# A three-layer graph network with an expert layer on one core: the last layer's work placed anew, two edge banks in place of three, and a bank for each half of an early slot's hidden product

## The reference, cut to what matters

```python
xn = layernorm(x)
h = xn
for l in range(3):
    agg = segment_sum(h[src], edge_type * N + dst, 8 * N).reshape(8, N, 256)
    h = act_l(einsum('rnd,rde->ne', agg, W[l]) + h @ root[l] + bias[l])   # relu, relu, sigmoid
x = x + h + linear_attention(xn)                                        # 4 heads of 32
y = layernorm(x)
top_p, top_idx = top_k(softmax(y @ Wr + br), 2)                          # 8 experts
yn = layernorm_no_affine(y)
e(y) = gelu((yn * ln_g[e] + ln_b[e]) @ W1[e] + b1[e]) @ W2[e] + b2[e]    # 256 -> 1024 -> 256
out = x + sum over the 2 chosen experts of weight * e(y)
```

## Time and profile before

| | us |
|---|---|
| median of 3 runs (3805.47 to 3815.09) | 3810.72 |
| the profiled execution | 3800.47 |
| its span, first to last instruction | 3798.7 |
| PE busy in the span | 2900.7 (76%) |
| POOL busy in the span | 2397.5 (63%) |
| DVE busy in the span | 1179.5 (31%) |
| ACT busy in the span | 447.0 (12%) |

### The profile page before, as it was taken

How to read it: one execution, slowest core, us unless ns; L and a number is a source line. 1 busy time by engine, 2 the same in 40 slices (tenths; PEclk the granted TensorE clock), 3 DMA queues, 4 the chain that set the end, 5 groups by cost and what they waited for, 6 DMA issues and landing times.

```text
span 3798.7 us, 51045 instructions
## 1 busy us (share of the span) xinstructions
PE 2900.7 (76%) x16228; PEld 2552.1 (67%) x16228; DVE 1179.5 (31%) x2813; ACT 447.0 (12%) x1220; POOL 2397.5 (63%) x2537
## 2 busy tenths in 40 slices
PE   3878777877778888888888778787767777777791
PEld 3776766776666676677666567776666666667791
DVE  5232223222232223222322233333332333333312
ACT  1000000000000000000000010122121211212230
POOL 5777777777757777777776677755445554543005
PEclk9888888898888778877878777798888888888896
DMA  7444444444443333333333333555444454544653
GB/s 175 133 146 132 133 146 133 132 136 143 133 131 110 108 108 109 108 108 108 109 107 100 116 105 105 161 167 160 143 139 159 142 160 137 156 147 133 216 187 112
DMA packets 272287, 511.76 MB, mean 135 GB/s; under 512 B 60237, under 2 KB 177119, under 8 KB 272032
## 3 DMA queue, kind: packets, MB, share of 16 engines
q0 software_dynamic: 120864, 330.20, 29.8%
q1 hardware_dynamic: 150000, 178.85, 14.8%
q10 hardware_dynamic: 1296, 1.24, 0.1%
HBM read 453.68 MB, written 56.42 MB: 134 GB/s over the span
## 4 chain that ended last, share of the span: by engine, by line
POOL 45%; PE 25%; issue 20%; DVE 4%; DVEq 2%; DMA 1%; ACT 1%; ACTq 1%; POOLq 0%; SPq 0%
POOL arena L590 44%; PE bank L1584 6%; PE bank L1530 4%; PE bank L1599 3%; PE bank L1643 3%; PE bank L1639 2%; PE bank L1777 2%; PE bank L1787 2%; POOL arena L655 1%; ACT arena L777 1%; PE bank L1523 1%; DVE arena L1193 1%; DVEq L1228 1%; DMA arena<-rows_dram,arena 0%; PE bank L1521 0%
## 5 line engine op out<-in xcount | busy, mean ns | idle before, releaser
L590 POOL DMA_INDIRECT arena<-rows_dram,arena x2396 | 2268.8, 947 | 906.7 <-issue 751.9
L1639 PE MATMUL bank<-arena 128*128 128x128 f32 x4836 | 1082.2, 331 | 436.0 <-DMA arena<-rows_dram,arena 374.9
L1639 PEld LDWEIGHTS bank<-arena 128*128 128x128 f32 x4836 | 855.3, 223 | 636.9 <-DMA arena<-rows_dram,arena 469.3
L1278 DVE TENSOR_TENSOR arena<-arena,bank 128x256 f32 x807 | 340.4, 422 | 2226.3 <-PE bank L1643 2123.2
L1643 PE MATMUL bank<-arena 128*128 128x128 f32 x4836 | 798.7, 310 | 0.0
L1643 PEld LDWEIGHTS bank<-arena 128*128 128x128 f32 x4836 | 732.1, 226 | 0.0
L1530 PE MATMUL bank<-arena 128*128 128x256 f32 x2400 | 600.3, 390 | 0.0
L1530 PEld LDWEIGHTS bank<-arena 128*128 128x128 f32 x2400 | 445.4, 198 | 49.2 <-issue 0.5
L1584 PE MATMUL bank<-arena 128*128 128x128 f32 x1152 | 220.2, 370 | 255.7 <-DVE arena L1152 171.0
L1584 PEld LDWEIGHTS bank<-arena 128*128 128x128 f32 x1152 | 207.7, 279 | 264.9 <-issue 264.9
L1211 DVE TENSOR_TENSOR arena<-bank,arena 128x1408 f32<-128x1408 f32 x222 | 355.3, 1603 | 13.0 <-issue 13.0
(11 more groups left out here) (204 smaller groups left out, 1373.0 us busy)
## 6 DMA issues: line engine op xcount, KB each, us to landing
arena<-in_L_ffn_W_dram SPq DMA_DIRECT2D x112, 512.0 KB, 4.3
arena<-in_L_ffn_W_dram SPq DMA_DIRECT2D x44, 1024.0 KB, 6.2
arena<-rows_dram,arena POOLq DMA_INDIRECT x2418, 2.8
xs_dram<-zrow SPq DMA_DIRECT2D x25, 1152.0 KB, 5.6
arena<-xs_dram SPq DMA_DIRECT2D x56, 128.0 KB, 2.1
xs_dram<-arena SPq DMA_DIRECT2D x56, 128.0 KB, 2.7
rows_dram<-arena SPq DMA_DIRECT2D x50, 128.0 KB
arena<-in_L_gnn_weights_dram SPq DMA_DIRECT2D x6, 1024.0 KB, 8.8
```

The costliest lines, as they stand in the source:

```text
L590: nc.gpsimd.indirect_dma_start(out=gath[:, slot, :], out_offset=None, in_=rows_dram[l], in_offset=bass.IndirectOffsetOnAxis(ap=idx_ring[:, ...
L1278: nc.vector.tensor_tensor(acc, acc, bank[EDGE_BANKS[q % 3]][:, 0:KD * WC].rearrange("p (k r n) -> p k r n", k=KD, r=REL), ALU.add).then_in ...
L1639: nc.tensor.matmul(bank[EDGE_BANKS[q % 3]][:, 0:WC], gath[:, slot, 0:P], onehot[:, slot, :], start=first, stop=last)
```

## The change

Four things are changed in the last layer, and one in all layers.

1. The tables place the work elsewhere. DVE's numbers now count groups (0 to 10, and 11 for behind the last), and its work stands ahead of that group's addition, no longer behind a tile's.
2. The last layer uses edge banks 0 and 1 in turn. Bank 2 becomes the bank of h1, bank 6 stays that of h0, and each half waits only for the same half of the slot before.
3. The output product of c = 0 goes to the left half of bank 5 and that of c = 1 to the right; the router's and the counts' results move from bank 5 to the turn bank 4. The waits follow.
4. `router` and `route` run in the same span as the node (behind tile 30, ahead of group 10), `dealt` and `route_pos` early in the next span.
5. In every layer the window offsets of a span are loaded into DVE's registers 4, 4 and 3 at a time, where 11 were loaded at once.

```diff
-STAGE, LAST_STAGE, POST, TURN, BACK = 4, 11, 17, 23, 26
+STAGE, LAST_STAGE, POST, TURN, BACK = 4, 11, 14, 23, 26
-X2, YN, XN2, DEV1, DEV2, YBACK, YTURN, ROUTE = 20, 23, 26, 21, 24, 28, 27, 1
+X2, YN, XN2, DEV1, DEV2, YBACK, YTURN, ROUTE = 5, 6, 7, 19, 19, 29, 27, 30
...
-RT, RT_MM, RT_POS = 5, 7, 11
-PICK, LAST_PICK = (14, 17), (13, 13)
-PLACE = (dict(turn=0, scale=2, h0=4, h1=8, out=16, bias=20), dict(turn=17, scale=20, h0=22, h1=25, out=29, bias=32))
+RT, RT_MM, RT_POS = 10, 2, 3
+PICK, LAST_PICK = (3, 4), (4, 4)
+LOADS = 4
+PLACE = (dict(turn=2, scale=0, h0=8, h1=15, out=22, bias=8), dict(turn=19, scale=6, h0=22, h1=29, out=32, bias=11))
...
-        E_HID, E_OUT = 6, 5
+        E_HID, E_OUT = (6, 2), 5
+        router_o = bank[TURN_BANK][:, D:D + EXP]
+        dealt_o = bank[TURN_BANK][:, D + 2 * EXP:D + 4 * EXP]
+        early_o = [bank[E_OUT][:, c * D:(c + 1) * D] for c in range(2)]
...
+        def turned_ahead(u):
+            return sum(at["turn"] < u for at in PLACE)
+        def edge_bank(l, s, q):
+            return bank[EDGE_BANKS[(q + s.par) % 2 if l == LAYERS - 1 else q % 3]]
...
@@ DVE, a span
+                            if q % LOADS == 0:
+                                n = min(LOADS, groups - q)
+                                wins += nc.values_load_multi_w_load_instructions(
+                                    win_row[0:1, bass.ds(SG * s.m + q, n)], engines=(dve.engine,), min_val=0, max_val=RING - 1,
...
+                            beside(q)
                             for u in us[:-1]:
                                 key(u)
                             wait(dve, "group_mm", g + 1)
                             wait(dve, "tile_add", g)
                             acc = agg[:, :, :, bass.ds(wins[q], WN)]
-                            nc.vector.tensor_tensor(acc, acc, bank[EDGE_BANKS[q % 3]]...
+                            nc.vector.tensor_tensor(acc, acc, edge_bank(l, s, q)...
-                                beside(u)
...
+                        beside(groups)
@@ PE
-            def early_turn(k, c, y):
+            def early_turn(k, c, y, signal):
                 s = 2 * k + c
                 pe.wait_ge(s_xe[c], 16 * (k + 1))
                 wait(pe, "e_back", s)
-                wait_apart(pe, "y_out", y)
+                wait(pe, "y_out", y)
+                wait_apart(pe, signal, y)
...
-                wait_apart(pe, "e_act", 2 * s + h)
+                wait_apart(pe, "e_act", 2 * s + h - 1)
...
-                                    wait(pe, "tile_add", GROUPS * l if is_first(s) and q < 3 else g - 1 if q < 2 else g - 2)
+                                    if final:
+                                        wait(pe, "tile_add", GROUPS * l if is_first(s) and q < 2 else g - 1)
+                                    else:
+                                        wait(pe, "tile_add", GROUPS * l if is_first(s) and q < 3 else g - 1 if q < 2 else g - 2)
```

More of the change, by code:

```diff
@@ L1227, in span @@
                         groups = -(-tiles // GT)
[L1228 to L1234, removed]
+                        wins = []
@@ new lines, in beside @@
+                        def beside(q):
+                            if final and early(s) is not None:
+                                for c in range(2):
+                                    if q == places(s)[c]["scale"]:
+                                        early_scale(early(s), c)
+                                    if q == places(s)[c]["bias"]:
+                                        early_bias(early(s), c, early_o[c])
+                            if not is_first(s) and q == READY:
+                                whole(l, t, (s.i,) if not s.par else (), GROUPS * l + SG * s.m + q)
+                            if not is_first(s) and not is_last(s) and q == ZERO:
+                                clean(l, t, place_of(t, s.par))
+                            if final and not is_first(s) and not is_last(s):
+                                if q == X2:
@@ L1235, in beside @@
                                     x2_node(t)
-                                if final and u == YN:
+                                if q == YN:
                                     y_node(t)
-                                if final and u == XN2:
+                                if q == XN2:
                                     xn2_node(t, 1 - s.par, t - 1)
[L1240 to L1244, removed]
+                                if q == RT:
+                                    route(t)
@@ L1245, in beside @@
+                            if final and not (is_first(s) or is_int(s.m, 1)) and q == RT_POS:
+                                route_pos(s.m - 2, s.par, s.m - 3)
                             if final and picks(s) is not None:
                                 for c in range(2):
-                                    if u == (LAST_PICK if is_last(s) else PICK)[c]:
+                                    if q == (LAST_PICK if is_last(s) else PICK)[c]:
                                         pick_slot(2 * picks(s) + c)
[L1249 to L1253, removed]
-                                        early_bias(early(s), c, early_o)
@@ L1255, in beside @@
-                            if l == 0 and u == PREP["bias"]:
+                            if l == 0 and q == PREP["bias"]:
                                 bias_in(s.m)
-                            if l == 1 and not is_first(s) and not is_last(s) and u == MIX_ADD:
+                            if l == 1 and not is_first(s) and not is_last(s) and q == MIX_ADD:
                                 mix_node(t)
```

81 lines of the change are left out of this document (37 added, 44 removed).

## The result

The median of the changed kernel's runs is 3463.18 us (3461.70 to 3463.78, and one run of 3543.67 that the comparison leaves out) against 3809.24 us before on the same chip: ratio 0.9089, 95% interval 0.9071 to 0.9107. The forecast was 3515 us in a range from 3450 to 3650. The change took away 346 us where 295 were forecast; the profiled execution has a span of 3460.7 us against 3798.7.

What follows compares the result with a forecast made beforehand. PE was taken to be held up by short chains through DVE and ACT, POOL following. (89.3 + 4) / 2 = 46.7 us a span; 45 + 794 = 839 for 18 intervals, 295 less: 3515 us, range 3450 to 3650.

Steps and rivals of the forecast that it cites:

- The scaled rows: Last layer, rows of c = 1 scaled ahead of group 6: PE's wait of 12.1 us a span goes.
- A bank for each half: Hidden product, last layer: h1 no longer waits for the gelu of h0; 3.1 us a span go.
- Router, counts, positions: Span ends and starts, last layer: PE's 2.0 us a span for counts go; POOL's 13.3 for `route_pos` shrink.
- Two edge banks: Edge additions, last layer: DVE's piles of work fit under PE's products; cost taken as 0.
- Rival C: DVE's piles ahead of groups 3 to 7 uncovered, PE waits: 69 us a span, 3895 us, slower; chance 0.05.
- Rival B: Last layer: half of PE's 17.6 us of waits remains, 57 us a span, 3690 us; chance 0.10.
- The loop's turn: DVE's 6.0 us stall at the loop's branch stays: 4.9 us a turn added, plus 3 for the lower clock.
- The gathers: POOL, last layer: floor of 43.9 us a span, 87.8 a turn; POOL over 85% busy as a sign.
- Rival D: DVE instructions lock POOL's port and slow gathers: floor 51 us, 3590 us; chance 0.21 together with rival A.
- Transfers: W1 and W2 loads, last layer, at 207 GB/s for 148: 1 us a span, between 0 and 5.
- Rival A: Last layer: transfers and clock bind, W1 lands late; 52 to 53 us a span, 3615 us; 0.21 with rival D.
- Two floors close together: PE's and POOL's turns, last layer, pass delays to each other: 2 us a span, between 0 and 6.

Runs made afterwards that it cites:

- The placing alone: Changed kernel with three edge banks and both hidden halves in bank 6 again, against the kernel before: 3461.87 us, 0.909; on another chip 4797.11 us, 0.967.

## Why the prediction was right, and where a size was off

*The scaled rows.* Right. 161.0 us became 0 outside the loop's turn.

*A bank for each half.* The wait went, as said, but the 3.1 us a span were credited to the bank in part. The placing alone has most of them too: without the second bank 0.7 us a time is left of the wait, and the time of that kernel is the same, since its third edge bank saves as much at the loop's turn. With the bank and without the placing, 31.2 of the 41.7 us came back at the output product. The seven tiles between h0 and h1 did most of it.

*Gelu ahead of the output product.* By hand 23.2 us against PE's 23.4; the wait is 0.17 us. Right within 0.4.

*Router, counts, positions.* Right: 26.1 us became 0, and POOL's 176.9 became 4.8.

*Two edge banks.* Right at 0 outside the turn: in the six turns PE waits for no addition but that of the turn, so the piles on DVE lie under PE's products. Rival C needed over 25 us a span of them. Rival B needed half of the 17.6 us a span of waiting; 2.9 are left.

*The loop's turn.* 4.9 us of waiting and 3 of lower clock were forecast; measured 33.0 / 6 = 5.5, and the span with the turn takes 48.0 - 40.1 = 7.9 more, which leaves 2.4 for the clock. The sum is right, its parts are off by 0.6 each way. That the stall belongs to the branch holds: DVE's branch is followed by 4.4 to 6.5 us without an instruction in each of the six turns, with the work in the new order, and by 4.8 to 5.6 in the old.

*PE's own span.* 39.7 forecast, 40.1 measured.

*The gathers.* POOL's turn was forecast at 87.8 and is 87.8. Rival D (DVE's work blocking POOL's port) isn't there: 946 ns either way. One bar was set wrong: "POOL over 85% busy" is not met at 481.81 / 640 = 75%, and could not be. A gather counts as 0.95 busy of its 1.25 us, so an engine at its floor shows 75% here, as layer 1 does (717.15 of 948).

*Transfers.* The size was off: 1 us a span forecast, nothing measured. W1's landing grew by 0.5 us in the median and by 0.6 at the slowest, at 1.5 times the traffic, and stayed inside the margin. Rival A, which scaled the landing time with the traffic, fails with that.

*Two floors close together.* The second size off: 2 us a span for "one passing its delays to the other", and hardly anything measured. The spans of PE go 40.1, 47.9, 40.1, 46.8 while POOL goes on evenly; the rows already gathered take up the difference. A turn takes 88.1 us, where the two engines' own turns were forecast at 87.3 and 87.8.

*The sum.* The forecast gave 839 us for the 18 intervals, the trace 797.1: 42 us. They are 17 x 2.64 = 44.9 for the later intervals (44.1 for 46.7) less 3.0 for the first interval, which took longer than forecast (48.0 for 45). The rest of the 52 us is that the profiled execution of before stood 10.2 us off its median and the one after 0.6 (9.6), and the 1.3 us at both ends (3.7 - 5.0), less 0.9 of rounding. The terms that were mis-sized are the two of safety, 3 us a span: without them the forecast for a turn was 87.3 to 87.8. The measured 3463 lies in the range, but 7 us below the 3470 to 3570 that had been given 0.62, and the starts are 44.1 us apart where 46 to 48 were to show it: the mechanism was right, the safety was too much.

## What to carry to other kernels

Count a removed wait only together with the next one on the same chain: a bank more, with the chain's parts still close together, moved 31.2 of 41.7 us elsewhere, while work placed between the parts left 0.7 of 3.2 us a time without the bank. When every engine's own work is summed from rows without waits, the largest of these sums was the time, within 0.3%, and the surcharge for two sums close together was not needed, since a queue of gathered rows lay between the engines. Measure such a change on more than one chip: the same edit, the placing alone, gave 9.1% on one and 3.3% on another. And before waits of two traces are compared, count their semaphore events: where two thirds are missing, as on three chips here, an idle engine seems to have had nothing to wait for.

## What was not expected of the hardware

The same kernel took 3807 to 3811 us on two occasions and 4870 to 4968 on three others, on different chips. The gathers were equally fast (0.95 us), and so was what follows the last node tile; in layer 1 DVE began its additions up to 16.3 us after their inputs were there, where 1.67 was the most on the chip of the forecast, and no run shows why. And DVE stands 6.0 to 6.8 us where the loop turns in the kernel before and 6.5 to 8.5 in the changed one. The branch makes most of it, 4.8 to 5.6 us before and 4.4 to 6.5 now, while the branches of ACT and POOL take up to 0.25 us in the same turns and PE shows no gap at its own.
